# A two-layer expert and attention kernel: low-order weight parts moved to VectorE ahead of the norm, loads spread over the blocks, the first shared step split behind attention

## Chip, cores and metric

One core of a Trainium2 chip runs the whole program in one launch. The metric is device microseconds (us) of one execution; a run's span is the time from the first to the last instruction in its trace.

## What is computed

The input x is 4 images of 16 x 16 positions with 192 channels, 1024 tokens in all. Cut to what matters:

```python
x = x + moe0(group_norm(x))       # 8 experts, 2 a token, inner size 512, GELU,
                                  # and a shared gated expert w1, w3, w2
t = to_tokens(x)
t = t + attention(layer_norm(t))  # 12 heads of 16, softmax twice with a mask
n = layer_norm(t)
t = t + shared(n) + routed(n)     # 16 experts, 2 a token, inner size 384, SiLU
```

Routing is exact: each token's two best experts by its logits, weighted by a softmax over the two. The group norm is over 6 channels and one image's positions.

## The kernel before

The kernel is written by hand as one instruction list for each engine (TensorE, VectorE, ScalarE, GpSimd, and SyncE, which issues loads); every dependence is a semaphore wait. Each engine works strictly in the order of its list, so the order of the code is the order of the work. Tokens lie in 8 tiles of 128.

**Head.** SyncE issues x_t, the averaging matrix, a part of the constants, the gate weights, then `w13` (1 MB, the two first weights of the shared expert; L544) and its biases `b13` (L545). Both of these count on one semaphore, `s_w13`, which is at 32 when both have landed. VectorE makes channel statistics (L910, L914); TensorE averages them over groups (`group_mean`, L1625) for the mean, VectorE forms the deviations (L916 to L919), TensorE averages again, VectorE takes the variance (L921), ScalarE the root (L790), and VectorE normalises x (L929, eight instructions). Where TensorE waits for that, it does matmuls without a use (`warm_up`, L1613).

The shared expert of layer 0 runs with operands that are split into a high part (the value cast to a narrower form) and a low part (the rest): `w13_high`, `w13_low`, `w13_stack` (64 rows that hold the high part of the last 64 channels and 64 with their low part), `x0_high`, `x0_low`. ScalarE makes the high parts (L792, L793, L798). Of the low parts of the weights, VectorE makes the first 128 columns and the stack (L600, L934), GpSimd the other three chunks (L600 called from L652); VectorE makes those of x (L941).

The shared expert's work is cut in steps (s, g): s counts the halves of the tokens and the chunks of 128 inner channels, g is 0 for the gate and 1 for the other factor. In layer 0 a step is 5 matmuls of 512 columns, in layer 1 it is 2 (L1451). The list `plan` (L481) says for both layers in which order TensorE and VectorE take these steps and the routing's own pieces: "logits", "count", "rank", "expert", "slots" on TensorE, "best0", "top2", "pads", "ended", "blocks", "places" on VectorE. Numbers in VectorE's list are its share of a step (the product of both factors, L1058).

**Blocks of layer 0.** 23 blocks of 128 gathered rows. For a block TensorE does `first` (L1517, 8 matmuls), the transposes of the next block's rows (L1494) and `second` of the block before (L1545). VectorE copies the weights of block b + 2 (`copy_weights`, L1179) and adds the bias to the result of block b (`result`, L1119); GpSimd gathers rows (L609) and scatters results (L617). After block 5 VectorE has two more pieces in a row: `w_low_parts` (L1092, L1097; low parts of the attention's weights) and the bias on the whole of `x_tok` (L1188). When the rows of the first blocks are there, SyncE issues eight loads without a further wait (L558 to L565): the attention's weights, x by token, two bias rows, w2, the second gate's weights and the shared weights of layer 1.

**Attention.** 24 pairs of heads; for a pair TensorE does scores, transposes of the attention (L1766) and weighted values (L1783), with `keep_busy` (one matmul of 256 columns, L1851) where it would wait. Behind the last pair stand the pieces of `chunk_stages`, the last projection (L1813), the transposes of the normalised tokens (`norm_transposes`, L1682), the logits of the first four tiles (L1419), the transposes of the other four, step (0, 0) of the shared expert and the logits of the other four:

```python
            for j in range(NT // 2):
                logits(L1, j)

            pe.wait_ge(x_new, IMAGES)
            norm_transposes(2, 1)
            shared(L1, 0, 0)
```

**Layer 1 and the end.** 31 blocks as in layer 0, with the shared expert's sums (`out_tile`, L1474) at the end. After the last scatter the results are brought back in four parts of two tiles (L524). Tiles in `OWN` are weighted and summed by VectorE (`add_own`, L1083), the others by TensorE (`add_experts`, L1486) and then added to x by VectorE (`add_tile`, L1069). Then two tiles at a time are stored (L592).

Of the kernel before, what the change touches and what calls it, by code (L numbers as in the profile page):

```python
# [145 lines left out]
def build(nc, d, out):  # L146
    with ExitStack() as ctx:
# [259 lines left out]
        w13_own_ready = sem("w13_own_low_ready")  # L407
# [57 lines left out]
        def image_at(p):  # L465
# [18 lines left out]
                ["w_low", "x_low0", "best0", "w_low_rest", "best1", "top2", 0, "pads", "x_low1", "ended", 1, "expert", "blocks", 2, "places", 3,  # L484
                 "slots", 4, "weights", 5, "first weights", 6, "diag0", 7, "diag1"]),
            1: ([(0, 1), (1, 0), "count", (1, 1), "rank", (2, 0), (2, 1), "expert", (3, 0), "slots", (3, 1), (4, 0),
# [10 lines left out]
        OWN = ((2, 3), (1, 3, 5))  # L497
        SUM_ORDER = ((2, 3, 0, 1, 4, 5, 6, 7), (1, 3, 5, 0, 2, 4, 6, 7))
# [39 lines left out]
        def _(sp):  # L538
# [36 lines left out]
            sp.wait_ge(x_biased, 1)  # L575
# [12 lines left out]
            for q in range(4):  # L588
                t = slice(q * NT // 4, (q + 1) * NT // 4)
                sp.wait_ge(L1.sum_ready, len(OWN[1]) + q + 1 if q < 3 else NT)  # L590
                sp.wait_ge(L1.own_sums, TOPK * min(q + 1, len(OWN[1])))
# [4 lines left out]
        def w13_low_part(eng, ic):  # L596


            chunk = slice(ic * P, (ic + 1) * P)
            return eng.tensor_tensor(w13_low[:, :, chunk], w13[:, 0, :, chunk],  # L600
                                     w13_high[:, :, chunk].bitcast(F32), ALU.subtract)
# [36 lines left out]
        def _(pool):  # L638
# [263 lines left out]
        def _(dve):  # L902
# [462 lines left out]
            for j in (6, 7):  # L1365
                add_tile(L1, j)
# [593 lines left out]
```

## Time and profile before

| | us |
|---|---|
| median of 3 runs | 429.67 |
| lowest and highest | 421.46 and 429.68 |
| the profiled execution | 426.82 |
| its span | 424.9 |
| TensorE busy in it | 395.0 |
| mean granted TensorE clock, share of full | 0.98 |

The table gives the profiled execution's own time beside its span: 1.9 us lie outside the first and last instruction. A share of the granted clock of 1.00 is 2.4 GHz, one of 0.50 is 1.2 GHz. Busy time of matmuls is modelled at their ends, so a start is read more safely than a duration.

### The profile page before, as it was taken

How to read it: one execution, taken by the hardware profiler on the slowest of the kernel's cores; microseconds unless marked ns; L12 is line 12 of the kernel's file. 1: busy time of each engine (PE TensorE's matmuls, PEld its weight loads, DVE VectorE, ACT ScalarE, POOL GpSimd, SP SyncE). 2: the span in 40 equal slices, each digit the busy share in tenths (PEclk: the TensorE clock that was granted, in tenths of full speed). 3: DMA queues.
4: the chain of work that ended last, by engine and by line, in shares of the span. 5: the costliest groups of instructions: out<-in, count | busy, mean ns of one | idle time of the engine just before them, and what ended most of it. 6: DMA issues, size and time to landing. Idle time of an engine off the chain costs nothing.

```text
span 424.9 us, 8481 instructions
## 1 busy us (share of the span) xinstructions
PE 395.0 (93%) x2513; PEld 321.3 (76%) x2514; DVE 272.0 (64%) x709; ACT 192.9 (45%) x480; POOL 129.5 (30%) x139
## 2 busy tenths in 40 slices
PE   8999999899999999888888869999899999999995
PEld 3788899799999877667676656555678888888884
DVE  3867634433322887988989766374687777777734
ACT  1625333122231276988888843133444454545410
POOL 2201366466644000000000000003255555555520
PEclk9969999999999999999999998699999999999999
DMA  9993192111104870000000598900111111110006
GB/s 309 207 339 153 37 294 85 45 50 45 34 10 148 248 338 2 0 2 2 1 2 2 133 257 226 264 1 12 34 38 41 35 43 50 42 32 24 0 0 224
DMA packets 17627, 40.42 MB, mean 95 GB/s; under 512 B 5743, under 2 KB 10805, under 8 KB 17122
## 3 DMA queue, kind: packets, MB, share of 16 engines
q1 hardware_dynamic: 9378, 30.64, 23.5%
q0 software_dynamic: 5280, 6.85, 5.5%
q10 hardware_dynamic: 2944, 2.62, 1.9%
q8 instruction: 13, 0.21, 0.2%
q14 instruction: 12, 0.10, 0.1%
HBM read 37.19 MB, written 7.93 MB: 106 GB/s over the span
## 4 chain that ended last, share of the span: by engine, by line
PE 74%; DVE 7%; ACT 7%; DMA 6%; issue 3%; DVEq 1%; ACTq 0%; POOL 0%; POOLq 0%
PE bank L1545 13%; PE bank L1522 9%; PE bank L1517 8%; PE bank L1451 6%; PE bank L1766 5%; PE bank L1447 4%; PE bank L1736 3%; PE bank L1783 3%; DMA w_first<-y_rows 3%; PE bank L1494 2%; PE bank L1533 2%; PE bank L1528 2%; PE bank L1527 2%; ACT scratch L855 2%; ACT xn_t L855 2%
## 5 line engine op out<-in xcount | busy, mean ns | idle before, releaser
L609 POOL DMA_INDIRECT rows<-xn_rows,slot_tok x56 | 58.6, 1047 | 110.9 <-DVE slot_tok L1044 54.8
L617 POOL DMA_INDIRECT y_rows<-y,slot_row x54 | 58.2, 1078 | 42.7 <-issue 19.0
L1545 PE MATMUL bank<-w_second,hid_t 128*128 x274 | 51.7, 327 | 0.7 <-DVE hid_t L1102 0.7
L1517 PE MATMUL bank<-rows_t,scratch 96*128 96x128 f32 (+1 forms) x368 | 45.3, 275 | 3.2 <-DVE scratch L1179 2.8
L1517 PEld LDWEIGHTS bank<-rows_t,scratch 96*128 96x128 f32 (+1 forms) x368 | 43.8, 191 | 4.5 <-DVE scratch L1179 2.4
L1522 PE MATMUL bank<-w_first,rows_t 128*128 x124 | 45.3, 488 | 0.4 <-issue 0.4
L1545 PEld LDWEIGHTS bank<-w_second,hid_t 128*128 128x128 f32 x274 | 43.5, 190 | 1.1 <-issue 1.0
L665 POOL COPY act_h<-o_inv 128x256 f32<-128x256 f32 x12 | 5.1, 425 | 116.5 <-DVE o_inv L1311 116.5
L738 ACT ACTIVATE act_g<-bank 128x384 f32<-128x384 f32 x31 | 15.2, 491 | 46.6 <-PE bank L1528 46.6
L1119 DVE TENSOR_TENSOR y<-bank,w_second 128x192 f32<-128x192 f32 x23 | 8.2, 357 | 40.7 <-PE bank L1545 35.9
L1275 DVE TENSOR_REDUCE neg_max<-bank 128x4 f32<-128x1024 f32 x24 | 28.9, 1203 | 1.4 <-PE bank L1715 1.3
L846 ACT ACTIVATE w_first<-bank,neg_max 128x256 f32<-128x256 f32 x64 | 29.4, 482 | 0.0
L1522 PEld LDWEIGHTS bank<-w_first,rows_t 128*128 128x128 f32 x124 | 21.2, 190 | 9.1 <-issue 0.9
L1301 DVE SCALAR_TENSOR_TENSOR w_first<-w_first,exp_inv,const 128x256 f32<-128x256 f32 x64 | 26.9, 482 | 0.6
L1102 DVE COPY hid_t<-bank 128x384 f32<-128x384 f32 x31 | 17.3, 557 | 15.0 <-PE bank L1533 10.3
L1451 PE MATMUL bank<-xn_t,sh 96*128 96x512 f32 x48 | 25.6, 681 | 0.0
L1179 DVE COPY scratch<-w_first 96x512 f32 (+1 forms) x46 | 17.6, 425 | 11.5 <-issue 10.7
L1107 DVE TENSOR_TENSOR act_h<-bank,act_g 128x384 f32<-128x384 f32 x31 | 17.3, 557 | 9.0 <-ACT act_g L738 8.6
L732 ACT ACTIVATE act_h<-bank 128x512 f32<-128x512 f32 x12 | 7.2, 597 | 31.9 <-PE bank L1517 31.9
L1494 PE MATMUL bank<-const,rows 128*128 128x128 f32 (+1 forms) x112 | 21.5, 273 | 0.1
L1545 PE MATMUL bank<-w_second,act_h 128*128 x96 | 17.7, 327 | 0.7 <-DVE y L1119 0.7
L732 ACT ACTIVATE hid_t<-bank 128x512 f32<-128x512 f32 x11 | 6.6, 597 | 25.8 <-PE bank L1517 25.8
(234 smaller groups left out, 887.2 us busy)
## 6 DMA issues: line engine op xcount, KB each, us to landing
w_first<-in_gate_up SPq DMA_DIRECT2D x16, 384.0 KB, 6.4
w_second<-in_down SPq DMA_DIRECT2D x1, 4608.0 KB, 18.3
w_first<-in_fc SPq DMA_DIRECT2D x1, 3072.0 KB
w_second<-in_fc SPq DMA_DIRECT2D x1, 3072.0 KB, 27.9
w_first<-in_gate_up_rest SPq DMA_DIRECT2D x16, 192.0 KB, 7.2
w_first<-in_x_t SPq DMA_DIRECT2D x2, 512.0 KB, 4.8
w_first<-in_w SPq DMA_DIRECT2D x1, 1024.0 KB, 6.4
w_first<-in_wqkv SPq DMA_DIRECT2D x1, 960.0 KB, 5.0
```

The lines of the kernel that those rows point to most:

```text
L609: pool.indirect_dma_start(rows[b % 2][:, 0:ROW[L.l]], None, xn_rows[L.l], bass.IndirectOffsetOnAxis(slot_tok[:, b:b + 1].bitcast(U32), 0), ...
L617: pool.indirect_dma_start(y_rows[L.l], bass.IndirectOffsetOnAxis(slot_row[:, b:b + 1].bitcast(U32), 0), y[b % 2][:], None, bounds_check=TO ...
L846: ins = nc.scalar.activation(e1[p % 3][:, q, :], bank[:, 2 * (p % 2) + q // 2, (q % 2) * 256:(q % 2 + 1) * 256], ACT.Exp, bias=neg_max[:, ...
L1179: v.tensor_copy(first_w[u][0:CH + k, k, :], w).then_inc(L.first_w_ready, 1)
L1275: v.tensor_reduce(neg_max[:, p % 4, :], bank[:, b:b + 2, :].rearrange("p b (a k) -> p (b a) k", a=2), AXX, ALU.max, negate=True).then_inc( ...
L1301: ins = v.scalar_tensor_tensor(e1[p % 3][:, q, :], e1[p % 3][:, q, :], exp_inv[:, p % 2, q:q + 1], mask, ALU.mult, ALU.mult)
L1451: ins = pe.matmul(bank[:, bk + s % 2, :], w[:, k, g, ic * P:(ic + 1) * P], xn_t[0:CH, k, t], start=(k == 0), stop=(k == NCH - 1))
L1494: ins = pe.transpose(bank[0:n, 0, tile(k)], rows[u][:, k * n:(k + 1) * n], ident)
L1517: ins = pe.matmul(bank[:, 5, tile(ic)], first_w[u][0:kr, k, tile(ic)], rows_t[0:kr, k, :], start=(k == 0), stop=(k == NCH - 1))
L1522: pe.matmul(bank[:, 5 + g, 0:I1], rows_t1, w(P, g * I1, I1), start=True, stop=False)
L1545: ins = pe.matmul(bank[:, 1, 0:C], hid[:, tile(ic)], w(P, ic * C, C), start=(ic == 0), stop=(ic == L.IC - 1))
L1766: ins = pe.transpose(bank[:, 4 + m, (kt * 2 + qt) * P:(kt * 2 + qt + 1) * P], e1[p % 3][:, 2 * m + qt, tile(kt)], ident)
```

## The change

Five edits, all to the order of the work and to who does it.

1. Head: ScalarE casts the high parts of w13 ahead of the root (first the stack, then `w13_high`). VectorE makes all low parts of w13: the stack's after the channel statistics and ahead of the mean, `w13_low` in two instructions ahead of the variance. GpSimd's three instructions and VectorE's three behind the norm are gone. All steps of TensorE wait for `w13_low_ready` at 3.
2. Loads: x by token and its bias wait for the fourth `second` of layer 0 (`y_ps`), w2 for the seventh, the other four for the ninth.
3. Blocks of layer 0: VectorE's two extra pieces are cut in four, which stand behind the results of blocks 5, 6, 7 and 8; ten blocks are written out ahead of the loop where six were.
4. Behind attention: three more `keep_busy` matmuls; step (0, 0) of layer 1 stands ahead of the first logits, and (0, 1) between the second transposes and the second logits. The list `plan[1]` begins one step later; "count", "rank", "expert" and "slots" each follow one step later in it.
5. End: VectorE's own tiles in layer 1 are 1, 3 and 7 where they were 1, 3 and 5, and it adds in the order own 1, tile 0, own 3, tiles 2, 4, 5, own 7, tile 6.

```diff
         @block.scalar
         def _(act):
 
+            act.wait_ge(s_w13, 32)
+            nc.scalar.copy(w13_stack[0:REST], w13[0:REST, 1]).then_inc(w13_high_ready, 1)
+            nc.scalar.copy(w13_high[:], w13[:, 0]).then_inc(w13_high_ready, 1)
             act.wait_ge(var_ready, 1)
             nc.scalar.sqrt(grp_rstd[:], grp_rstd[:]).then_inc(std_ready, 1)
-            act.wait_ge(s_w13, 32)
-            nc.scalar.copy(w13_high[:], w13[:, 0]).then_inc(w13_high_ready, 1)
-            nc.scalar.copy(w13_stack[0:REST], w13[0:REST, 1]).then_inc(w13_high_ready, 1)
...
                 v.bn_aggr(chan_mv[:, n, :], chan_stats[:, n, :]).then_inc(chan_ready, 1)
+
+            dve.wait_ge(w13_high_ready, 1)
+            v.tensor_tensor(w13_stack[REST:], w13[REST:, 1], w13_stack[0:REST].bitcast(F32), ALU.subtract
+                            ).then_inc(w13_low_ready, 1)
             dve.wait_ge(gmean_ps, 1)
...
             v.tensor_tensor(chan_dev[:], chan_dev[:], chan_mv[:, :, 1], ALU.add).then_inc(dev_ready, 1)
+            dve.wait_ge(w13_high_ready, 2)
+            for g in range(2):
+                v.tensor_tensor(w13_low[:, g], w13[:, 0, g], w13_high[:, g].bitcast(F32), ALU.subtract
+                                ).then_inc(w13_low_ready, 1)
             dve.wait_ge(gvar_ps, 1)
...
-            for ic in range(1, I0 // P):
-
-                pool.wait_ge(xn_t_ready, NCH * IMAGES)
-                pool.wait_ge(w13_high_ready, 1)
-                w13_low_part(nc.gpsimd, ic).then_inc(w13_low_ready, 1)
...
             sp.dma_start(wqkv, d["wqkv"]).then_inc(s_qkvw, 16)
+
+            sp.wait_ge(L0.y_ps, 4)
             sp.dma_start(x_tok[:], by_tile(d["x"])).then_inc(x_tok_in, 16)
             sp.dma_start(w2_b, d["w2_b"]).then_inc(x_tok_in, 16)
+            sp.wait_ge(L0.y_ps, 7)
             sp.dma_start(w2, d["w2"]).then_inc(s_sh0, 16)
+            sp.wait_ge(L0.y_ps, 9)
...
-                for b in range(6):
+                for b in range(10):
                     copy_weights(L, b + 2, b % 2)
                     result(L, b, b % 2, b // 2)
-                w_low_parts()
-                dve.wait_ge(x_tok_in, 32)
-                v.tensor_tensor(x_tok[:], x_tok[:], bc(w2_b, 1, [P, NT, C]), ALU.add).then_inc(x_biased, 1)
-
-                with dve.Fori(0, (L.NB - 9) // 2) as i:
+                    if b in (5, 6):
+                        w_low_part(b - 5)
+                    if b in (7, 8):
+
+                        t = slice((b - 7) * NT // 2, (b - 6) * NT // 2)
+                        dve.wait_ge(x_tok_in, 32)
+                        v.tensor_tensor(x_tok[:, t], x_tok[:, t], bc(w2_b, 1, [P, NT // 2, C]), ALU.add
+                                        ).then_inc(x_biased, 1)
...
-            for j in OWN[1]:
-                add_own(L1, (j,))
-                add_tile(L1, j - 1)
-            for j in (6, 7):
-                add_tile(L1, j)
+
+            for own, js in ((1, (0,)), (3, (2, 4, 5)), (7, (6,))):
+                add_own(L1, (own,))
+                for j in js:
+                    add_tile(L1, j)
...
             chunk_stages(N_PAIRS)
+            keep_busy(1)
             chunk_stages(N_PAIRS + 1)
+            keep_busy(1)
             project_last(tuple(range(HC - 1)))
...
+            shared(L1, 0, 0)
             for j in range(NT // 2):
                 logits(L1, j)
 
             pe.wait_ge(x_new, IMAGES)
             norm_transposes(2, 1)
-            shared(L1, 0, 0)
+            shared(L1, 0, 1)
```

VectorE in the head, from the channel averages to the low part of x. Before (chan_mv are the channels' means and variances, grp_mean and grp_rstd the groups', xn_t the normalised x):

```order
L914 BN_AGGR chan_mv<-chan_stats 128x2 x8
L916 COPY grp_mean<-bank 128x8
L917 TENSOR_TENSOR chan_dev<-chan_mv,grp_mean 128x8
L918 TENSOR_TENSOR chan_dev<-chan_dev 128x8
L919 TENSOR_TENSOR chan_dev<-chan_dev,chan_mv 128x8
L921 TENSOR_SCALAR grp_rstd<-bank 128x8
L924 RECIPROCAL grp_rstd<-grp_rstd 128x8
L929 TENSOR_SCALAR xn_t<-w_first,grp_mean,grp_rstd 128x256 x8
L600 TENSOR_TENSOR w_low<-w_first,w_high 128x2x128
L934 TENSOR_TENSOR w_stack<-w_first,w_stack 64x2x128
L941 TENSOR_TENSOR x_low<-xn_t,x_high 128x512 x2
```

The same place of VectorE's list now:

```order
L906 BN_AGGR chan_mv<-chan_stats 128x2 x8
L909 TENSOR_TENSOR w_stack<-w_first,w_stack 64x1024
L912 COPY grp_mean<-bank 128x8
L913 TENSOR_TENSOR chan_dev<-chan_mv,grp_mean 128x8
L914 TENSOR_TENSOR chan_dev<-chan_dev 128x8
L915 TENSOR_TENSOR chan_dev<-chan_dev,chan_mv 128x8
L918 TENSOR_TENSOR w_low<-w_first,w_high 128x512 x2
L921 TENSOR_SCALAR grp_rstd<-bank 128x8
L924 RECIPROCAL grp_rstd<-grp_rstd 128x8
L929 TENSOR_SCALAR xn_t<-w_first,grp_mean,grp_rstd 128x256 x8
L936 TENSOR_TENSOR x_low<-xn_t,x_high 128x512 x2
```

The subtractions on w13 have moved from behind the norm into the chain that leads to it, and the first one stands ahead of the mean.

TensorE behind attention, from the last projection to "count" (L1379 before, L1372 now). Before (sh are the shared expert's weights, gate the gate's, const the identity):

```order
L1813 MATMUL bank<-w_first 128x192 x2
L1682 MATMUL bank<-const,xn_tok 96x128 x8
L1851 MATMUL bank<-const 128x256 x2
L1419 MATMUL bank<-gate,xn_t 128x16 x8
L1682 MATMUL bank<-const,xn_tok 96x128 x8
L1451 MATMUL bank<-xn_t,sh 128x512 x2
L1419 MATMUL bank<-gate,xn_t 128x16 x8
L1451 MATMUL bank<-xn_t,sh 128x512 x4
L1379 MATMUL bank<-ones,before 16x1
```

The same place of TensorE's list now:

```order
L1804 MATMUL bank<-w_first 128x192 x2
L1673 MATMUL bank<-const,xn_tok 96x128 x8
L1842 MATMUL bank<-const 128x256 x2
L1442 MATMUL bank<-xn_t,sh 128x512 x2
L1412 MATMUL bank<-gate,xn_t 128x16 x8
L1673 MATMUL bank<-const,xn_tok 96x128 x8
L1442 MATMUL bank<-xn_t,sh 128x512 x2
L1412 MATMUL bank<-gate,xn_t 128x16 x8
L1442 MATMUL bank<-xn_t,sh 128x512 x4
L1372 MATMUL bank<-ones,before 16x1
```

One step (two matmuls of 512 columns) has moved ahead of the first logits, and four steps instead of three stand ahead of "count".

## Rows read from the trace of the kernel before

**Rows 1.** The page: granted clock of TensorE in 40 equal slices, in tenths of full.

```profile
PEclk9969999999999999999999998699999999999999
```

**Rows 2.** Windows: stretch and length, busy us and instructions of each engine, granted clock, DMA.

```profile
20.95:27.80 6.85, 6.85 (x25) 5.95 (x25) 2.90 (x22) 1.55 (x3) 0.00 (x0) 0.50 0.97 291
...
250.00:263.30 13.30, 11.44 (x87) 9.29 (x88) 8.66 (x44) 5.18 (x10) 0.81 (x2) 1.00 0.87 234
263.30:273.50 10.20, 10.20 (x25) 6.09 (x24) 3.52 (x26) 2.25 (x3) 0.00 (x0) 0.50 1.04 284
```

**Rows 3.** Timeline of the head: start, us, engine, line, operation, idle before and its releaser.

```profile
9.77 0.17 DVE L916 COPY grp_mean<-bank 128x8 f32<-128x8 f32 x1 [1.21 <-PE bank L1625]
...
11.51 2.40 PE L1613 MATMUL bank<-ones 128*128 128x256 f32 x10
...
12.37 2.67 DVE L929 TENSOR_SCALAR xn_t<-w_first,grp_mean,grp_rstd 128x256 f32<-128x256 f32 x8
12.94 1.04 ACT L793 CAST w_stack<-w_first 64x1024 fp32r<-64x1024 f32 x1
...
13.90 1.92 PE L1419 MATMUL bank<-gate,xn_t 128*128 128x8 f32 x16
...
18.66 0.47 PE L1447 MATMUL bank<-x_high,w_high 128*128 128x512 f32 x1 [1.01 <-DVE x_low L941]
...
19.73 0.95 DVE L934 TENSOR_TENSOR w_stack<-w_first,w_stack 64x768 fp32r<-64x768 f32 x1
```

**Rows 4.** Timeline of SyncE's queue: the issue of b13.

```profile
4.03 0.43 SPq L545 DMA_DIRECT2D b<-in_b  x1
```

**Rows 5.** DMA issues: the same load, its size and us from issue to landing.

```profile
b<-in_b SPq DMA_DIRECT2D x1, 4.0 KB, 6.2
```

**Rows 6.** TensorE's timeline in the blocks of layer 0: `first` of blocks 2, 3 and 8.

```profile
53.20 1.95 PE L1517 MATMUL bank<-rows_t,scratch 96*128 96x128 f32 x16
...
56.51 1.95 PE L1517 MATMUL bank<-rows_t,scratch 96*128 96x128 f32 x16
...
76.63 2.05 PE L1517 MATMUL bank<-rows_t,scratch 96*128 96x128 f32 x16 [2.09 <-DVE scratch L1179]
```

**Rows 7.** VectorE's timeline between the results of blocks 5 and 6.

```profile
72.89 1.22 DVE L1097 TENSOR_TENSOR w_high<-w_first,w_high 64x480 fp32r<-64x480 f32 x2
74.15 1.76 DVE L1188 TENSOR_TENSOR x_tok<-x_tok,w_second 128x1536 f32<-128x1536 f32 x1
```

**Rows 8.** The chain of waits in the blocks: start, us, what.

```profile
56.22 5.97 DMA rows<-xn_rows,slot_tok
```

**Rows 9.** The gathers' line, L609, over the whole span: time to landing.

```profile
DMA to landing us min/median/max: 2.1/2.7/3.3
```

**Rows 10.** TensorE's timeline behind attention.

```profile
258.72 1.03 PE L1851 MATMUL bank<-const 128*128 128x256 f32 x4
259.59 1.93 PE L1419 MATMUL bank<-gate,xn_t 96*128 96x16 f32 x16
261.92 1.13 PE L1682 MATMUL bank<-const,xn_tok 128*96 128x128 f32 x8 [0.41 <-DVE xn_tok L1218]
262.89 3.20 PE L1451 MATMUL bank<-xn_t,sh 96*128 96x512 f32 x4
...
274.94 0.20 PE L1379 MATMUL bank<-ones,before 128*16 128x1 f32 x2
275.07 1.98 PE L1451 MATMUL bank<-xn_t,sh 96*128 96x512 f32 x4
276.89 0.39 PE L1389 MATMUL bank<-scan,const 128*128 128x128 f32 x2
```

**Rows 11.** Timeline of the end, VectorE and TensorE.

```profile
419.47 0.87 DVE L1083 SCALAR_TENSOR_TENSOR x_tok<-w_first,weight,x_tok 128x192 f32<-128x192 f32 x2
419.58 2.58 PE L1486 MATMUL bank<-w_first,scratch 128*128 128x192 f32 x12 [0.49 <-DMA w_first<-y_rows]
...
422.19 0.35 DVE L1069 TENSOR_TENSOR x_tok<-x_tok,bank 128x192 f32<-128x192 f32 x1 [0.30 <-PE bank L1486]
```

More of the change, by code:

```diff
@@ L483, in build @@
                  "expert", (2, 1), (3, 0), (3, 1), (4, 0), (4, 1), "slots", (5, 0), (5, 1), (6, 0), (6, 1), (7, 0), "first rows", (7, 1)],
-                ["w_low", "x_low0", "best0", "w_low_rest", "best1", "top2", 0, "pads", "x_low1", "ended", 1, "expert", "blocks", 2, "places", 3,
+                ["x_low0", "best0", "best1", "top2", 0, "pads", "x_low1", "ended", 1, "expert", "blocks", 2, "places", 3,
                  "slots", 4, "weights", 5, "first weights", 6, "diag0", 7, "diag1"]),
-            1: ([(0, 1), (1, 0), "count", (1, 1), "rank", (2, 0), (2, 1), "expert", (3, 0), "slots", (3, 1), (4, 0),
+            1: ([(1, 0), (1, 1), "count", (2, 0), "rank", (2, 1), (3, 0), "expert", (3, 1), "slots", (4, 0),
                  (4, 1), (5, 0), (5, 1), "first rows", "out0", "out1"],
@@ L574, in _ @@
                 load_expert(sp, e)
-            sp.wait_ge(x_biased, 1)
+            sp.wait_ge(x_biased, 2)
             sp.dma_start(w_second[:], d["down"]).then_inc(s_w1b, 16)
@@ L589, in _ @@
                 t = slice(q * NT // 4, (q + 1) * NT // 4)
-                sp.wait_ge(L1.sum_ready, len(OWN[1]) + q + 1 if q < 3 else NT)
-                sp.wait_ge(L1.own_sums, TOPK * min(q + 1, len(OWN[1])))
+                sp.wait_ge(L1.sum_ready, max(sum_no(L1, j) for j in (2 * q, 2 * q + 1)))
+                sp.wait_ge(L1.own_sums, TOPK * len([j for j in OWN[1] if j < 2 * q + 2]))
                 sp.dma_start(by_tile(out)[:, t], x_tok[:, t]).then_inc(out_done, 16)
             sp.wait_ge(out_done, 16 * 4)
[L596 to L601, printed above, removed]
         def pool_blocks(pool, L):
@@ L930, in _ @@
                                     grp_rstd[:, n:n + 1], ALU.subtract, ALU.mult).then_inc(xn_t_ready, 1)
-            def stack_low_part(start, end):
-                v.tensor_tensor(w13_stack[REST:, :, start:end], w13[REST:, 1, :, start:end],
-                                w13_stack[0:REST, :, start:end].bitcast(F32), ALU.subtract).then_inc(w13_own_ready, 1)
             def x_low_part(half):
@@ L1085, in add_own, with w_low_part @@
                                                ).then_inc(L.own_sums, 1)
-            def w_low_parts():
-                for q in range(2):
+            def w_low_part(of):
+                for q in range(2) if of == 0 else ():
                     dve.wait_ge(w_high_ready, 1)
@@ L1093, in w_low_parts @@
                                     ).then_inc(w_low_ready, 1)
-                for q in range(2):
+                for q in range(2) if of == 1 else ():
                     dve.wait_ge(w_high_ready, 2)
@@ L1182, in blocks @@
                 dve.wait_ge(s_fc2b, 16)
[L1183 removed]
+                for b in range(10):
                     copy_weights(L, b + 2, b % 2)
                     result(L, b, b % 2, b // 2)
[L1186 to L1190 removed]
+                    if b in (5, 6):
[5 more added lines that the diff above has]
+                                        ).then_inc(x_biased, 1)
+                with dve.Fori(0, (L.NB - 13) // 2) as i:
                     for u in range(2):
[L1192 removed]
+                        b = i * 2 + (u + 12)
                         copy_weights(L, b, u)
[L1194 removed]
+                        result(L, b - 2, u, i + 5)
                 copy_weights(L, L.NB - 1, (L.NB - 1) % 2)
@@ L1437, in shared @@
                     if half == 0:
-                        pe.wait_ge(w13_own_ready, 3 if ic else 2)
-                        if ic:
-                            pe.wait_ge(w13_low_ready, ic)
+                        pe.wait_ge(w13_low_ready, 3)
                     if ic == 0 and g == 0:
@@ L1844, in chunk_stages, with keep_busy @@
                     project(image_at(p))
-            def keep_busy(n):
+            def keep_busy(n, free=4):
                 for _ in range(n):
-                    pe.matmul(bank[:, 4, 0:TOKENS_IMG], ident, mask, start=True, stop=True)
+                    pe.matmul(bank[:, free, 0:TOKENS_IMG], ident, mask, start=True, stop=True)
             for p in range(N_PAIRS):
@@ L1860, in _ @@
                     chunk_stages(p)
+                    keep_busy(1, 1)
                     continue
```

15 lines of the change are left out of this document (3 added, 12 removed).

## The prediction

> **What bounds the kernel now.** I read the page first. TensorE is busy for 395.0 of 424.9 us, and most of the chain that ended last are its matmuls, so in most stages a microsecond counts only if it is taken from TensorE's list or from what that list waits for. The row of the granted clock [rows 1] shows two places that differ from the rest: the third slice and the two slices at three quarters of the span. The windows [rows 2] give their length: 6.85 us from 20.95 on and 10.20 us from 263.30 on at 0.50, which is 1.2 GHz; everywhere else the clock is 2.4 GHz. The reader is to see that TensorE is never idle in either of them: it only runs at half speed, and each place costs up to half its length. I then read the timeline of the head [rows 3], the blocks of layer 0 [rows 6 to 8], the place behind attention [rows 10] and the end [rows 11], because the change touches these and no others.
>
> The three runs themselves are 8.2 us apart (421.46 to 429.68). The two low stretches can cost 3.4 and 5.1 us, half of 6.85 and 10.20 [rows 2], 8.5 in all. As an estimate, then, the spread of the runs is that of the clock, and which low stretches a run has is part of its time. I work against the profiled execution, 426.82 us (span 424.9 and 1.9 around it), which has both. It lies 2.85 below the median of 429.67, so my sum may be low by as much if a typical run has more low clock than the profiled one.
>
> **Head, the order.** VectorE's first subtraction now stands ahead of the mean and needs ScalarE's cast of the stack, which needs w13 and b13. b13 is issued at 4.03 [rows 4] and lands 6.2 later [rows 5], at 10.2. The cast takes 1.04 [rows 3] and ends at 11.3. Before, the copy of the mean started at 9.77 [rows 3]. The subtraction of 1024 columns is not in the trace; one of 768 took 0.95 [rows 3], so I take 0.95 x 1024/768 = 1.2 (1.0 to 1.7). The mean is copied at 12.5, 2.75 late. The two subtractions of w13_low (2 x 512 columns, another 1.2) stand ahead of the variance, but beside TensorE's second averaging of about as long; 0.2 of them sticks out. So normalising starts at 12.37 + 2.95 = 15.3 and ends at 18.0 [rows 3], and the first logits move from 13.90 to 16.8. Behind them TensorE has the logits, one matmul without use and eight transposes, 3.75 us up to the 1.01 us for which it waited for the low part of x [rows 3]. Now that wait is covered: with step (0, 0) at 16.8 + 3.75 = 20.5 instead of 18.66, **+1.8**. The low part of x is then ready by 19.4. Queued behind VectorE's new wait is the whole norm, and TensorE, ScalarE and GpSimd all wait for that. If w13 came early enough the term would be 0, if 1 us later 2.8. Removing GpSimd's three instructions gives nothing here, since nobody waits for them then.
>
> **Head, the clock.** No row shows what the new wait of 2.7 us does to the clock. Before, TensorE lost it at 20.95, after a stretch of logits with 8 columns, transposes and the wait of 1.01 [rows 3]. Now a longer wait stands at 10.7 to 13.4, with one matmul without use ahead of it. If the clock falls there, the 2.40 us of matmuls without use [rows 3] and some 1.9 us of filler and transposes take twice as long, +4.3. Against this the later fall, of 3.4, may then not come, since TensorE is dense from 20.5 on. The ends are -3.4 (no fall in the head at all) and +4.3 (both falls). I take one fall in place of the other, 4.3 - 3.4 = **+1.0**, since nearly everything that led to the old fall is still there.
>
> **Blocks of layer 0.** Blocks 2 and 3 start 3.31 apart, blocks 2 and 8 23.43 apart [rows 6]; six at 3.31 are 19.86, so 3.57 are lost. Of these 2.09 are TensorE's wait for the weights that VectorE copied late [rows 6], behind 1.22 + 1.22 + 1.76 us of extra work in a row [rows 7]; L1092 takes as long as L1097. Those 4.2 us in one block cost 2.09, so a block has room for 2.1; pieces of 0.9 to 1.2 fit into it. So **-2.1** (-2.3 to -1.5). The remaining 1.5 are loads: a gather took 5.97 us [rows 8] with all eight loads just issued, where the median is 2.7 [rows 9]. The attention's weights still come at once; the rest comes in three parts. I take **-0.8** (-1.5 to 0). What is late next is TensorE itself, which is the bound of these blocks. SyncE's queue waits in all three places for blocks of layer 0 that end long before its next item, the return of the results.
>
> The row of the slow gather (5.97, rows 8) can be set against the Trainium skill, "DMA: Bandwidth & Descriptors", section "Queues, rings and completion order": an engine serves its queue rows in turn, packet by packet. By that rule a gather is delayed by any load beside it, however much is queued behind, and three smaller bursts delay gathers in three places; the -0.8 would then be 0, and the sum 423.2. The row fits either reading.
>
> **Behind attention, the clock.** From 262.89 to 274.94 TensorE did one step, the second logits and two steps [rows 10], 12.05 us. At full clock a step takes 276.89 - 275.07 = 1.82 and eight logits 1.93 [rows 10], together 7.4. So the low clock cost 4.7. In the 13.3 us ahead of the fall TensorE was idle for 1.9 [rows 2], and much of the rest were transposes, logits of 16 columns and sums of 4. The change fills idle time with three matmuls and, above all, sets a step of 512 columns between fillers and logits, and another between transposes and logits, so that no long run of thin work is left. I take the fall as gone, **-4.7** (-5.1 to 0).
>
> **Behind attention, the order.** Two fillers took 259.59 - 258.72 = 0.87 [rows 10], so one is 0.44. The first falls into a wait for ScalarE; the other two lie in TensorE's list, +0.9. The 0.41 of waiting ahead of the second transposes [rows 10] is covered by step (0, 0), -0.4. The steps are only moved. "count" comes one step (1.8) later in time, but has one step less behind it, and the list shifts "slots" with it, so four instead of five steps lie behind "slots" until the first block; they last 7.3 us, and a gather needs 1 + 2.7 [rows 9]. Net **+0.4** (0 to 1.8).
>
> **End.** Tiles 6 and 7 were both TensorE's after the last part had landed; three tiles take it 2.58 [rows 11], so one less is up to -0.9. In exchange VectorE's pair of 0.87 [rows 11] stands ahead of its last addition: up to +0.9. I take 0.
>
> **Sum.** 426.82 + 1.8 + 1.0 - 2.1 - 0.8 - 4.7 + 0.4 = **422.4 us**. That is 1.7% below the median. A measurement of this kernel can tell about 2% from no change, so the likeliest case reads as no change.
>
> **Rivals.**
> - The clock falls behind attention all the same. For it: fillers stood there before, and the logits and transposes are as many. Against it: the steps between them. Then the -4.7 goes: 427.1. The wait right ahead of the old fall was only 0.41 us [rows 10]. The Trainium skill, "TensorE: Matmul & The Clock Gate", section "HAM oscillation — how this bites in real kernels", puts the loss of the clock down to long waits of the engine; by that, covering waits of this size changes nothing, which is this rival's time. The trace does not agree, since it has falls with no long wait ahead.
> - The head costs no clock: fillers on both sides of the new wait hold it and TensorE is dense behind it. Then -3.4 instead of +1.0: 418.0.
> - Slower: the fillers are too thin in both places, so that the clock is low from the new wait on, again at 20.5 or later, and behind attention. 426.82 + 1.8 + 4.3 - 2.9 + 0.4 = 430.4. It decides from the point at which two falls in the head and the one behind attention stand in one trace.
> - The change does not do what it says behind attention: with the logits 1.8 us later, VectorE's routing becomes what TensorE waits for at "slots". 422.4 + 1.8 = 424.2.
>
> **How the numbers follow.** Forecast 0.42, its own range 420 to 424.5; clock falls behind attention 0.22; free head 0.20; slower 0.08; routing bound 0.08. The range of 417.0 to 428.5 leaves out most of the slower case and the edges of two others, under 0.2. Faster by over 2% is below 421.1: all of the free head and a quarter of the forecast, 0.32. Slower by over 2% would be above 438.3 against the median, or above 429.9 against the fastest run; I give it 0.05. Within 2%: 0.63.
>
> **What would show it.** In the new profile: the copy of the mean at 12.5 and step (0, 0) at 20.5 or later; a low clock between 13 and 25; blocks of layer 0 with no wait for VectorE and 3.31 apart throughout; a clock of 1.00 from 250 on; TensorE without a wait at "slots". I am wrong if the mean is copied before 11, if the clock is low behind attention, or if the blocks still lose over 1.5 us.

## The result and the profile after

| us | changed | before, measured beside it |
|---|---|---|
| median of 4 executions each | 431.72 | 427.15 |
| lowest and highest | 429.44 and 433.94 | 421.46 and 429.68 |
| profiled execution (span) | 430.14 (428.0) | 426.82 (424.9) |

The ratio is 1.020, with a 95% interval of 1.015 to 1.026: the change makes the kernel slower; whether by 2% stays unclear. This ratio and all below leave out executions over 1.5% above the fastest of the same kernel, here the two of before at 429.67 and 429.68, so that it is larger than that of the medians (1.011). I had forecast 422.4 and a range of 417.0 to 428.5. The prediction was wrong, in its sign too.

I read the granted clock first, from the page, then from the windows (stretch, length, busy us and instructions of TensorE, its weight loads, VectorE, ScalarE, GpSimd; clock; DMA).

```profile
PEclk9699999999999999999999999978999999999999
```

```profile
12.88:19.71 6.83, 6.48 (x21) 5.58 (x21) 5.72 (x16) 3.00 (x7) 0.00 (x0) 0.50 0.99 216
277.80:280.71 2.91, 0.04 (x2) 0.00 (x1) 2.85 (x7) 0.00 (x0) 0.00 (x0) 1.00 0.00 0
...
282.53:292.77 10.24, 10.24 (x26) 6.11 (x25) 2.20 (x8) 0.60 (x1) 2.10 (x2) 0.50 0.05 14
```

Both low stretches of before [rows 2] are still there in number and length, at 1.2 GHz: the one in the head comes 8 us earlier, the one at 263.30 now comes at 282.53. Ahead of the second stands a stretch of 2.91 us that was not there before, in which TensorE does next to nothing (0.04 us) and VectorE is busy throughout.

The head, in its timeline (start, us, engine, line, operation, idle before and its releaser):

```profile
10.08 1.04 ACT L782 CAST w_stack<-w_first 64x1024 fp32r<-64x1024 f32 x1 [8.06 <-DMA b<-in_b]
...
11.16 1.22 DVE L909 TENSOR_TENSOR w_stack<-w_first,w_stack 64x1024 fp32r<-64x1024 f32 x1 [2.83 <-ACT w_stack L782]
...
12.41 0.17 DVE L912 COPY grp_mean<-bank 128x8 f32<-128x8 f32 x1
...
13.23 1.87 PE L1616 MATMUL bank<-chan_dev,w_first 128*128 128x4 f32 x8 [2.58 <-DVE chan_dev L915]
14.96 4.61 PE L1604 MATMUL bank<-ones 128*128 128x256 f32 x10
...
19.37 2.01 PE L1412 MATMUL bank<-gate,xn_t 128*128 128x8 f32 x16
...
22.97 0.47 PE L1438 MATMUL bank<-x_high,w_high 128*128 128x512 f32 x1
```

The order is as forecast: cast, subtraction, mean at 12.41. The matmuls without use last 4.61 us instead of 2.40 [rows 3], since the clock has fallen in between. Step (0, 0) starts at 22.97 instead of 18.66.

The blocks of layer 0, in TensorE's timeline:

```profile
68.05 2.02 PE L1508 MATMUL bank<-rows_t,scratch 96*128 96x128 f32 x16
...
71.99 2.05 PE L1508 MATMUL bank<-rows_t,scratch 96*128 96x128 f32 x16 [0.28 <-issue]
...
96.28 2.02 PE L1508 MATMUL bank<-rows_t,scratch 96*128 96x128 f32 x16 [0.86 <-ACT rows_t L717]
```

The wait of 2.09 for copied weights [rows 6] is gone. Two blocks come late instead: the one at 71.99 comes 3.94 after the one ahead of it instead of 3.31, and the one at 96.28 waits for rows that ScalarE copied late.

Behind attention, TensorE's timeline:

```profile
258.58 1.03 PE L1842 MATMUL bank<-const 128*128 128x256 f32 x4
259.44 1.95 PE L1442 MATMUL bank<-xn_t,sh 96*128 96x512 f32 x4
...
270.92 0.20 PE L1372 MATMUL bank<-ones,before 128*16 128x1 f32 x2
...
277.63 0.21 PE L1391 MATMUL bank<-ended,ones 16*1 16x32 f32 x2
280.71 2.01 PE L1442 MATMUL bank<-xn_t,sh 96*128 96x512 f32 x4 [2.87 <-DVE scratch L1056]
282.13 3.82 PE L1400 MATMUL bank<-in_blk,at_place 128*128 128x32 f32 x16
285.79 10.58 PE L1442 MATMUL bank<-xn_t,sh 96*128 96x512 f32 x16
...
299.38 1.45 PE L1513 MATMUL bank<-w_first,rows_t 128*128 x4
```

"count" (L1372) is 4.0 us earlier than before [rows 10] and the clock is 1.00 up to here, as forecast. All of that and 2.2 more is lost between "expert" (L1391) and the first block. What TensorE waits for is in VectorE's timeline, the last row here, its product of step 1:

```profile
276.04 0.69 DVE L1021 TENSOR_TENSOR eq_blk<-const,slot_f 128x512 f32<-128x512 f32 x1
276.77 0.69 DVE L1024 TENSOR_TENSOR in_blk<-eq_blk,const 128x512 fp32r<-128x512 f32 x1
277.38 2.49 DVE L1030 TENSOR_TENSOR at_place<-const,slot_f 128x512 fp32r<-128x512 f32 x4
279.79 0.27 DVE L1017 TENSOR_SCALAR blk_weights<-bank 1x32 int32<-1x32 f32 x2
279.99 0.67 DVE L1056 TENSOR_TENSOR scratch<-bank,g_sh 128x512 f32<-128x512 f32 x1
```

Step (3, 1) writes the bank that this product reads. It stands behind "blocks" and "places" in VectorE's list. In the kernel before the same wait was in the code but never reached in time, as its timeline of both engines shows:

```profile
281.65 0.21 PE L1398 MATMUL bank<-ended,ones 16*1 16x32 f32 x2
281.80 1.98 PE L1451 MATMUL bank<-xn_t,sh 96*128 96x512 f32 x4
283.22 2.26 PE L1407 MATMUL bank<-in_blk,at_place 128*128 128x32 f32 x16
...
284.01 0.67 DVE L1061 TENSOR_TENSOR scratch<-bank,g_sh 128x512 f32<-128x512 f32 x1
...
285.32 8.83 PE L1451 MATMUL bank<-xn_t,sh 96*128 96x512 f32 x20
```

There the step behind "expert" is (3, 0), and (3, 1) starts at 285.32, behind "slots", when the product (284.01 and 0.67) is done.

The end, in VectorE's timeline:

```profile
421.93 0.35 DVE L1064 TENSOR_TENSOR x_tok<-x_tok,bank 128x192 f32<-128x192 f32 x1
423.58 0.35 DVE L1064 TENSOR_TENSOR x_tok<-x_tok,bank 128x192 f32<-128x192 f32 x1 [1.29 <-PE bank L1477]
...
424.50 0.87 DVE L1078 SCALAR_TENSOR_TENSOR x_tok<-w_first,weight,x_tok 128x192 f32<-128x192 f32 x2
425.28 0.35 DVE L1064 TENSOR_TENSOR x_tok<-x_tok,bank 128x192 f32<-128x192 f32 x1
```

The pair of tile 7 now stands ahead of the last addition.

**The stages compared.** From here on I cut every trace at the same five starts of TensorE: the first `first` of layer 0, the first `out_tile` of layer 0, the last transpose of an attention, the first `first` of layer 1, the last `second`; the last column goes to the end of the span. Each number is a difference of two starts. "Low" is the low clock in the trace: start and length.

| trace | head | blocks 0 | attention | behind | blocks 1 | end | low clock |
|---|---|---|---|---|---|---|---|
| before | 46.79 | 81.88 | 122.40 | 46.11 | 113.04 | 14.71 | 21.0 (6.8), 263.3 (10.2) |
| changed | 48.30 | 80.19 | 122.02 | 48.87 | 113.00 | 15.64 | 12.9 (6.8), 282.5 (10.2) |

Head +1.5, blocks -1.7, attention -0.4, behind +2.8, end +0.9: together +3.1, which is 428.0 less 424.9.

### The profile page after: what moved, and what is told of

The parts are those of the page before. It is cut to its first block, busy times and chain, and to the rows that moved or that the text cites. A ratio compares the mean times of both kernels' runs of the same rounds, so it can differ in the third digit from the quotient of the medians.

```text
span 428.0 us, 8471 instructions
## 1 busy us (share of the span) xinstructions
PE 396.2 (93%) x2519; PEld 322.2 (75%) x2520; DVE 271.3 (63%) x710; ACT 194.5 (45%) x481; POOL 128.1 (30%) x136
## 4 chain that ended last, share of the span: by engine, by line
PE 78%; ACT 7%; DVE 5%; DMA 5%; issue 2%; SPq 1%; DVEq 1%; ACTq 0%; POOLq 0%
PE bank L1536 14%; PE bank L1508 10%; PE bank L1513 9%; PE bank L1757 5%; PE bank L1442 5%; PE bank L1727 3%; PE bank L1774 3%; PE bank L1438 3%; DMA w_first<-y_rows 3%; PE bank L1485 3%; PE bank L1524 2%; PE bank L1519 2%; PE bank L1518 2%; ACT xn_t L847 2%; ACT g_sh L847 2%
## 5 line engine op out<-in xcount | busy, mean ns | idle before, releaser
L614 POOL DMA_INDIRECT y_rows<-y,slot_row x54 | 59.2, 1096 | 38.6 <-issue 21.9
L1508 PEld LDWEIGHTS bank<-rows_t,scratch 96*128 96x128 f32 (+1 forms) x368 | 43.8, 190 | 3.2 <-issue 1.9
L1442 PEld LDWEIGHTS bank<-xn_t,sh 96*128 96x128 f32 x48 | 9.8, 217 | 13.6 <-issue 10.4
```

The lines of the kernel that those rows point to most:

```text
L614: pool.indirect_dma_start(y_rows[L.l], bass.IndirectOffsetOnAxis(slot_row[:, b:b + 1].bitcast(U32), 0), y[b % 2][:], None, bounds_check=TO ...
L1442: ins = pe.matmul(bank[:, bk + s % 2, :], w[:, k, g, ic * P:(ic + 1) * P], xn_t[0:CH, k, t], start=(k == 0), stop=(k == NCH - 1))
L1508: ins = pe.matmul(bank[:, 5, tile(ic)], first_w[u][0:kr, k, tile(ic)], rows_t[0:kr, k, :], start=(k == 0), stop=(k == NCH - 1))
```

## The experiments

Theory A is what the traces suggest: step (3, 1) was moved ahead of "slots" and so in front of a product that VectorE makes late; the wait, and the clock that falls behind it, cost what was lost. The rivals: the thin matmuls of "slots" cost the clock anyway (B), or the loss is the head's (C).

**1. The product ahead (e1).** In VectorE's list for layer 1 of the changed kernel:

```diff
-                ["best0", "best1", "top2", "pads", 0, "ended", "blocks", "places", "expert", 1, "slots", 2, 3,
+                ["best0", "best1", "top2", "pads", 0, "ended", 1, "blocks", "places", "expert", "slots", 2, 3,
```

> The changed kernel with VectorE's product of step 1 set directly behind "ended" in its list for layer 1; nothing else. Theory A (the new order makes step (3,1) wait for this product, 2.87 us in the changed kernel at 277.8, and that wait costs the clock at 282.5): step (3,1) starts at about 277.8 with no wait, "slots" at about 280.6 instead of 282.1, the clock stays at 1.00 from 250 to 300, and the time is 430.1 - 1.5 - 4.7 = about 424. Theory B (the clock falls there because of the thin work of "slots", with or without the wait): the wait is gone, the fall at about 282 stays, about 428.6. Theory C (the loss sits in the head): 430, no change.

Measured: 419.24 (418.35 to 423.21), 0.996 of before (0.993 to 1.000). TensorE's timeline:

```profile
275.42 0.21 PE L1391 MATMUL bank<-ended,ones 16*1 16x32 f32 x2
275.56 1.98 PE L1442 MATMUL bank<-xn_t,sh 96*128 96x512 f32 x4
276.98 2.26 PE L1400 MATMUL bank<-in_blk,at_place 128*128 128x32 f32 x16
279.09 7.11 PE L1442 MATMUL bank<-xn_t,sh 96*128 96x512 f32 x16
```

The wait and the fall are gone, and the stage behind attention takes 40.94 instead of 48.87. B falls: "slots" without the wait costs no clock, here and in the traces of e5, e6, e11, e13, e15 and e17, which have the same line. A is right in kind; its gain in this stage is 7.9 and not the 6.2 that I wrote, since "slots" did not have to wait for the routing either. The spans of the two profiles are 11.1 apart (428.0 and 417.0); the rest, 1.9 in the blocks of layer 0, 0.9 at the end and 0.6 in the head, lies where this run edits nothing, and is not its gain.

**2. The list not shifted (e2).** The changed kernel with

```diff
-            1: ([(1, 0), (1, 1), "count", (2, 0), "rank", (2, 1), (3, 0), "expert", (3, 1), "slots", (4, 0),
+            1: ([(1, 0), "count", (1, 1), "rank", (2, 0), (2, 1), "expert", (3, 0), "slots", (3, 1), (4, 0),
```

> The changed kernel in which "count", "rank", "expert" and "slots" stand behind the same steps as in the kernel before, with one step less ahead of each than in the changed kernel. Theory A: no wait for the product of step 1 (step (3,1) stands behind "slots"), but "count" now waits some 1.7 us for VectorE and "slots" some 0.9; total waiting like the 2.87 but in two pieces; about 427 if these pieces do not cost the clock. Theory B: a fall at "slots" as well, about 430. If the clock falls right behind the wait at "count" (before 282), any wait of this length is enough, wherever it stands.

Measured: 420.97 (420.48 to 426.84), 1.001 (0.997 to 1.006). TensorE waits ahead of "count":

```profile
268.90 0.20 PE L1372 MATMUL bank<-ones,before 128*16 128x1 f32 x2 [1.70 <-DVE before L971]
```

The stage takes 42.63, so 1.7 more than in e1, which is this wait; the one at "slots" did not come. In this profile the clock stays at 1.00 behind attention: a wait of 1.70 between steps of 512 columns cost no clock, the one of 2.87 ahead of one step and "slots" did. Three of the ten executions (425.19 to 426.84) had a lower mean clock than the others, at a place that no trace shows.

**3. Behind attention alone (e3), and the head undone (e4).** The kernel before with edit 4 only; the changed kernel with the head of before (edit 1 undone).

> The kernel before with the edit behind attention alone. Theory A: "count" 4.0 us earlier, then the wait of about 2.9 ahead of step (3,1) and a fall of the clock behind it, so the first block of layer 1 comes 2.8 us later than in the kernel before; about 429.6 against 426.8 of its profiled execution, ratio 1.007. My prediction's terms for this edit (-4.7 + 0.4) would give 422.5. Theory C (loss in the head): 422.5 as well.

> The changed kernel with the head of the kernel before. Theory A: blocks of layer 0 start 1.5 us earlier and all else is as in the changed kernel with its fall at 282: 430.1 - 1.5 = 428.6. Theory C: the head carries the loss, 424 or less; the clock's low stretch at 13 to 20 goes and one at 21 comes back (or none).

Measured: e3 430.61, 1.021 (1.016 to 1.027); e4 423.34, 1.008 (1.005 to 1.012). The stage behind attention takes 48.87 and 48.86, as in the changed kernel, with the wait (2.86) and the low stretch of 10.24. Edit 4 alone is as slow as the whole change, though its blocks keep their old wait and have two low stretches of 3.4 us in this profile. C is a smaller part, but not nothing: without the new head the ratio is 1.2 points lower than the changed kernel's 1.020, and 0.6 lower than its 1.015 in e16 below.

**4. The wait filled, not removed (e14), beside the changed kernel again (e16).**

```diff
                 stage(L1, s)
+                if s == "expert":
+                    keep_busy(6, 6)
```

> The changed kernel with its lists as they are, and six matmuls without use (256 columns, 0.43 us each) behind "expert", where TensorE waits 2.87 us for the product of step 1. The wait stays in time, only the idle time is filled. Theory A1 (it is the idle time together with the thin "slots" that costs the clock): no fall at 282, step (3,1) at the same time, about 5 us less than e16_after_again. Theory B ("slots" is thin enough alone): the fall stays, same time as e16.

> The changed kernel once more, on the same chip as the three others. Theory A: the fall behind step (3,1) is there in this profile too, and every execution has a mean clock of at most 0.98; 429 to 434, about 1.02 of before. If 282 was an accident of one execution, part of the runs is at 425 or less.

Measured: e14 421.91 (421.23 to 423.74), 1.001 (0.997 to 1.004); e16 428.30 (427.88 to 431.17), 1.015 (1.010 to 1.020). The fall at 284 is in e16 too; it is in all four traces with the shifted list and an unfilled wait (changed, e3, e4, e16). TensorE's timeline of e14:

```profile
275.16 2.86 PE L1842 MATMUL bank<-const 128*128 128x256 f32 x12
278.10 1.98 PE L1442 MATMUL bank<-xn_t,sh 96*128 96x512 f32 x4
279.51 2.26 PE L1400 MATMUL bank<-in_blk,at_place 128*128 128x32 f32 x16
281.62 7.11 PE L1442 MATMUL bank<-xn_t,sh 96*128 96x512 f32 x16
```

Step (3, 1) is as late behind "expert" as in the changed kernel (3.08 us in both), but "slots" takes 2.26 and not 3.82: no fall. The other executions agree: all 23 of the four kernels with the unfilled wait have a mean clock of 0.988 or less, all ten of e14 have 0.991 or more. This splits the loss: 48.87 (changed), 43.86 (wait filled), 40.94 (no wait). The clock costs 5.0 us and the wait itself 2.9. That the low clock follows idle time is what the Trainium skill says of it ("TensorE: Matmul & The Clock Gate", section "HAM oscillation — how this bites in real kernels": long waits re-throttle the engine). The waits in its example are longer than this one of 2.87 us, so the traces agree on the kind of cause and not on the length, and they do not agree for the fall of before at 263.30, right ahead of which TensorE waited only 0.41 [rows 10].

**5. The edit behind attention, repaired, on the kernel before (e15).** Edit 4 and the line of e1.

> The kernel before with the edit behind attention and with the product of step 1 behind "ended" in VectorE's list. Without the second edit (e3) this was 1.021 of before. Theory A: the wait and the fall go, and 'count' stays 4 us earlier or, where the kernel before has no fall at 263, equal: ratio 0.99 to 1.00, its profile without a low stretch between 250 and 300. If something else in the edit costs, 1.01 or more.

Measured: 421.74 (418.45 to 424.59), 0.998 (0.994 to 1.002). The stage takes 40.95. That it is no gain over before is explained by the next run.

**6. The kernel before again (e12).**

> The kernel before once more, for a second profile of it. Its runs go from 419 (clock 1.00) to 428 (0.98). If the fall behind attention at 263 is a habit of this kernel, it is in this profile too; if not, it is absent and the 4.7 us that my prediction took from it were there only in some executions.

Measured: 430.28. Its windows:

```profile
10.96:24.62 13.66, 13.66 (x46) 11.23 (x46) 8.61 (x28) 6.71 (x11) 2.83 (x3) 0.50 0.99 216
79.23:82.64 3.41, 3.41 (x19) 3.39 (x18) 0.54 (x2) 0.22 (x1) 1.02 (x1) 0.50 0.08 28
266.96:277.20 10.24, 10.24 (x25) 6.11 (x24) 3.51 (x26) 2.24 (x3) 0.00 (x0) 0.50 1.04 276
```

The fall behind attention is here too, and one in the blocks. But in three of the other traces whose code behind attention is that of before (e8, e9, e10, below) it is absent, and the stage takes 41.12 instead of 46.11. It is there in three of six (before, e12, e18). So the 4.7 that I took off is paid by some executions and not by others. Of 83 executions of the kernel before that were taken beside these runs (two more, at 664 and 2198 us, left out), 57 have a mean clock of 0.99 or more and take 419 to 424 us. A fall of 10.24 us alone brings the mean to 0.988, and only 26 of the 83 have that or less.

**7. The blocks: both edits (e8), VectorE's work cut (e9), the loads spread (e10).** The kernel before with edits 2 and 3, with 3, with 2.

> The kernel before with the loads spread and VectorE's extra work in the blocks of layer 0 cut in four; nothing else. My prediction's terms: -2.1 - 0.8 = -2.9, ratio 0.993, no wait for VectorE's weights in blocks 6 to 9. The rival is that each of the three bursts of loads delays gathers and gives back the 0.8 or more: the profile of the changed kernel shows -1.7, ratio 0.996.

> The kernel before with VectorE's extra work in the blocks of layer 0 cut in four and the loads as before. My prediction's term: -2.1, the wait of 2.09 for copied weights gone. If the loads were the limit all along, the wait only changes its name and this gives under 0.5.

> The kernel before with the loads spread and VectorE's work as before. My prediction's term: -0.8 (-1.5 to 0). Together the two gave blocks of 79.2 us (from the first `first` to the shared sums of layer 0) against 81.9. If the loads carry the most of it, this one shows over -1.5. A rival: x by token now lands later than VectorE's piece wants it, and the wait for the weights becomes longer than 2.09.

| run | median | ratio to before | blocks 0 | low clock in the blocks |
|---|---|---|---|---|
| e8 | 415.98 | 0.986 (0.976 to 0.996) | 79.17 | none |
| e9 | 418.93 | 0.994 (0.988 to 0.999) | 79.69 | none |
| e10 | 420.81 | 0.999 (0.992 to 1.005) | 82.55 | 73.5 (3.4) |

```profile
72.28 2.72 PE L1521 MATMUL bank<-rows_t,scratch 96*128 96x128 f32 x16 [2.09 <-DVE scratch L1183]
```

This row of e10, TensorE's timeline, is the wait for copied weights, which stays with the loads alone, and behind it the clock falls. Against 81.88 the cut is worth 2.2, and the loads another 0.5 (79.20 again in e18). The wait seems to cost the clock as well: of five traces that have it, four (e3, e10, e12, e15) have a low stretch of 3.4 us that begins 0.3 to 1.7 us after the block that waited; of the 14 others that can be read, none has a low stretch in the blocks. But e3 and e15 have a second one 15 to 16 us before this wait, at 61.8 and 61.2, and no run fills the wait, so that it is the cause here is not shown.

**8. The head alone (e7).** The kernel before with edit 1.

> The kernel before with the head edit alone. Theory A: the mean waits for w13, the clock falls in every execution at about 12, and the blocks of layer 0 start at 48; that is +1.5 against an old head with a fall and +4 against one without, so ratio 1.004 to 1.010 and the low stretch at 21 absent. My prediction's terms (+1.8 +1.0) say +2.8, 1.007. If VectorE's longer list in front of the norm is hidden behind the loads, 1.000.

Measured: 426.76, 1.010 (0.997 to 1.024), which by itself cannot be told from 1. Its profiled execution took 995 us, and nothing is read from it. What the head is worth is told better by e5 below, which differs from e1 in the head alone: 0.983 against 0.996.

**9. The new head filled (e11, e13).** On top of e1, six and then three more matmuls without use between the two averagings:

```diff
-            warm_up(1, 4 * P)
+            warm_up(4, 4 * P)
```

> The changed kernel with the product of step 1 behind "ended" and six more matmuls without use (512 columns) between TensorE's two averagings, where it was idle for 2.58 us. Theory: the idle time costs the clock at 12, which costs about 2.5 us on top of the new order; so the low stretch goes, the blocks of layer 0 start at 45.5 instead of 47.7, and the time is 418.9 - 2.2 = 416.7. If the order alone costs it, 418.9 as e1_product_first; if the fall only moves behind the logits of 8 columns, blocks start at 47 or later.

> As e11_head_filled, with three more matmuls of 512 columns instead of six: six took 5.2 us and pushed the second averaging from 13.3 to 15.4. Three take 2.6, the length of the idle time. Theory (clock and order each have a price in the head): no low stretch at 12, second averaging at about 13.2, blocks of layer 0 start at about 45.3, so 1.3 behind the old head without a fall (44.0) and 2.4 ahead of e1; about 416.7. If the clock falls all the same, 47.7 and 419.

Measured: e11 419.16 (0.996, 0.992 to 0.999), e13 417.11 (416.12 to 417.37; 0.988, 0.983 to 0.993). TensorE's timeline of e13:

```profile
9.40 3.68 PE L1604 MATMUL bank<-ones 128*128 128x512 f32 x8
13.30 1.05 PE L1616 MATMUL bank<-chan_dev,w_first 128*128 128x4 f32 x8 [0.22 <-DVE chan_dev L915]
...
16.61 1.92 PE L1412 MATMUL bank<-gate,xn_t 128*128 128x8 f32 x16
```

In e11 I had taken one such matmul for 0.43 us; it takes 3.68/4 = 0.92, so six overran the gap (second averaging at 15.42, blocks from 47.41 on) and gave the gain back. With three the clock holds and blocks start at 45.43. The old head starts them at 43.8 to 44.5 in eight of twelve traces, without a fall or with one of 3.4 us that costs nothing visible. So the new order costs 1.4 (45.43 against 44.0) and the clock the rest: 1.6 to 7.0 in the five traces with the unfilled new head (47.01 to 52.40), all of which have the fall.

**10. What is best (e5, e6, e17, e18).** e5 is the changed kernel with the old head and the line of e1; e6 has the old end as well; e17 is e5 again, e18 is e8 again.

> The changed kernel with the head of the kernel before and VectorE's product of step 1 behind "ended". Theory A adds the two repairs: the product alone gave 418.95 in its profiled execution, and the old head starts the blocks of layer 0 at 44.0 instead of 47.7 when it has no low clock, so 415.2; ratio about 0.985. If the old head has its fall at 21 in this kernel, 46.8 and 418. If the parts do not add (a freed clock in the head brings a fall elsewhere), 419 or more.

> As e5_old_head_product_first, and the end of the kernel before as well (own tiles 1, 3, 5). In the two profiles the time from the last `second` to the last addition is 11.96 before and 12.90 after. Theory A: the new order of the end costs 0.9, so this runs 0.9 us under e5. My prediction's term (0 in sum) : the same as e5 within 0.3.

> The same kernel as e5_old_head_product_first, in more rounds. Theory A: between 414.5 and 415.5 in nearly every execution, clock 1.00, since no place of it costs the clock; ratio 0.98 to 0.985.

> The same kernel as e8_only_blocks, on the same chip. It lacks the edit behind attention. Where its clock stays at 1.00 it should equal e17 within 0.5 us (e15 shows the repaired edit at nothing, 0.998); over all executions it should spread up to 420 and more, since nothing was done for the clock behind attention. If the repaired edit is worth something by itself, its fastest executions are over 1 us above those of e17.

| run | median | ratio to before | spread |
|---|---|---|---|
| e5 | 414.77 | 0.983 (0.974 to 0.993) | 414.66 to 415.50 |
| e6 | 415.11 | 0.988 (0.976 to 1.000) | 414.62 to 420.07 |
| e17 | 416.37 | 0.984 (0.980 to 0.987) | 414.97 to 421.44 |
| e18 | 422.83 | 0.993 (0.987 to 0.999) | 417.16 to 430.69 |

e5 beats the kernel before by 1.7% (e17 by 1.6%) and the changed one by more. e6 is the same within 0.4. e17 against e18, on one chip, tells what the repaired edit behind attention is worth (with the new end, which e6 shows to be worth nothing): its stage is only 0.2 faster (40.9 against 41.12) where neither has a fall, but the trace of e18 has two (246.81 with 6.83 and 260.46 with 10.24) and takes 48.93 there, while no trace of a repaired list with the new fillers has any. By my own sign, over 1 us between the fastest executions, it is worth something by itself (417.16 and 414.97); on the chip of e5 and e8 the fastest are 0.2 apart (414.66 and 414.90), so that stays open. My expectation for e17, nearly all at 414.5 to 415.5, was too tight: the old head still loses its clock in some executions (10.95 to 24.61 in this profile).

## Why the prediction was wrong

- **What failed: "The steps are only moved … the list shifts 'slots' with it"**, priced at +0.4 (0 to 1.8). I counted which steps lie behind "slots" and not what each moved step waits for. The shift set step (3, 1), which needs VectorE's product of step 1, ahead of "slots", while VectorE's list was left as it was. In the trace of before the product starts at 284.01, takes 0.67, and the step behind "expert" starts at 281.80: 2.9 us short, to be read there and then. The term measured +2.9 for the wait and, with the clock behind it, +7.8 (48.87 against 41.12 of a trace without a fall). The line of e1 takes both away (40.94).
- **Behind attention, the clock, -4.7 (-5.1 to 0).** The fall at 263.30 did go, and its size was right: 46.11 less 41.12 is 5.0. It came back at 282.53 at the same price. And the old fall is in three of six traces with that code, so the -4.7 held for the profiled execution, but for the kernel it was some 2.5 by the traces and 1.6 or less by the executions (26 of 83), both estimates; the new fall is in four traces of four, and the mean clock of all 23 executions fits it. That the three runs were 8.2 us apart had told me so, and I used it as a remark and not as a weight.
- **The rival "routing bound"** (chance 0.08) named the right engine, VectorE, and a place close by, "slots", but priced a bare delay of 1.8 and no clock. The slower rival (0.08) wanted two falls in the head and one behind attention and came to 430.4; the measured 430.14 of the profiled execution lies there by chance, with one fall in the head and a wait that this rival does not have.
- **Head, the order, +1.8.** Right in kind: the cast ends at 11.12 (forecast 11.3) and the mean is copied at 12.41 (12.5). The normalising starts at 15.82 instead of 15.3, since the second averaging ran at the low clock (1.87 us against 1.05 in e13). By e13 the term is +1.4.
- **Head, the clock, +1.0.** One fall took the place of the other, as I took it, but at no extra cost: both last 6.83 us, and between the two profiles the head is +1.5 in all, where order and clock together were forecast at +2.8. But the old head pays nothing for its clock in eight of twelve traces, and the new one, unfilled, pays in all five. Against these eight the head costs 3.0 to 4.3 in four of the five (47.01 to 48.30 against 44.0) and 8.4 in e16 (52.40). Same error as above: one execution stood for all.
- **Blocks, -2.1 and -0.8.** Right: -2.2 and -0.5 by e9 and e8. In the changed kernel's profile it was -1.7, because two blocks came late, for a cause that I did not settle; with the same edits it is -3.4 to -3.6 in e1, e2, e4, e5, e6, e14 and e16 and -2.3 to -2.8 in e11, e13 and e17, and that spread of over 1 us, which e5 and e17 show for one and the same kernel, is not explained either. Missing was the clock that seems to go with the removed wait. The rule of the Trainium skill that I set beside it ("DMA: Bandwidth & Descriptors", section "Queues, rings and completion order": an engine serves its queue rows in turn) would, as I read it, have made the -0.8 a 0; the interval of the runs cannot separate 0.5 from 0, only the blocks' stage hints at it.
- **End, 0 (±0.9).** +0.9 in the two profiles, but over all traces the old end takes 14.33 to 14.76 and the new one, apart from this one, 14.49 to 15.01; so 0 stands, and the 0.9 is that execution's.
- **The chances.** The 0.32 for faster by over 2% is 0.305 by its own terms (0.20 and a quarter of 0.42); nothing hangs on it.

The sum with measured terms, between the two profiled executions: 426.82 + 1.5 - 1.7 - 0.4 + 2.8 + 0.9 = 429.9, against 430.14. It only adds up the differences of the stages. Against the forecast of 422.4 the stage behind attention is 7.1 off (+2.8 instead of -4.3), nearly the whole miss of 7.7; the other misses, head -1.3, blocks +1.2, attention -0.4 and end +0.9, nearly cancel.

## What to carry to other kernels

When a step is moved in a fixed order, look up every semaphore that it waits for, find its producer's start in the trace, and compare that with the step's new start; a wait that never bit is still in the code, and shifting one engine's list without the other's is how it is met. Where a low clock in one profiled execution carries a term, weigh it by how many executions have it. And a wait of TensorE next to thin work may cost nearly twice its length again through the clock: filling it alone gave 5.0 us back in this stage (e14), removing it another 2.9 (e1).

## What the hardware showed that I had not expected

- The clock's fall costs more than the idle time that brings it on: 5.0 us behind a wait of 2.87, in four traces of four, and none where the same wait was filled (e14); 1.70 idle between steps of 512 columns cost none (e2).
- The same instructions keep the clock in one execution and lose it in another. Of twelve traces with the old head, six have no fall, two have one of 3.4 us, two of 6.8 and two of 13.7. The new head loses it in five of five traces, and with fillers in its wait (e11, e13) in none: every execution of these two has a mean clock of 0.999 to 1.00.
- A matmul without use of 512 columns takes 0.92 us and one of 256 columns 0.48 (2.86/6 in e14). The steps of layer 1 go at the same rate (1.82 for two of 512 columns), while a matmul of 512 columns on the split operands of layer 0 takes 0.23 from one start to the next, a quarter, as TensorE's timeline of e13 shows:

```profile
20.66 0.40 PE L1438 MATMUL bank<-x_high,w_low 128*128 128x512 f32 x1
20.89 0.40 PE L1438 MATMUL bank<-x_high,w_stack 128*128 128x512 f32 x1
```
